# Graph network kernel: one-hots made a group ahead in the linear passes, group entries loaded early, and the first histogram made from two digits

## The chip, the cores and the metric

One core of a Trainium2 chip runs the whole program in one launch. The metric is device time in microseconds. The engines are PE (TensorE, matrix products), DVE (VectorE), ACT (ScalarE), POOL (GpSimd, which here mostly issues indirect DMAs) and SP (SyncE, which here issues plain DMAs). They run apart and meet at semaphores.

## The reference, cut to what matters

A graph of 12500 nodes (64 features each) and 200000 edges with one of 33 types and a weight passes through four networks in a row, each followed by a residual and a layer norm:

```
x = layernorm(x + L0(x, relations, edges, types))   # hyperbolic, 2 hops
x = layernorm(x + L1(x, edges, weights))            # GRU, 2 rounds
x = layernorm(x + L2(x, edges))                     # SAGE, 2 convolutions
x = layernorm(x + L3(x, edges))                     # SAGE, 2 convolutions
```

Each hop, round and convolution gathers the row of one end of every edge and adds it up at the other end (`segment_sum(x[row], col)`). In L0 the row goes through a chain of hyperbolic maps first; in the others it is only summed, and what is linear is done on the sums. Dst is sorted, src isn't.

## The kernel before, in words

**Sort.** The program first sorts the edges by the block of 128 nodes of their head, once by src (k = 0) and once by dst (k = 1). There are NB = 98 blocks. `make_hist` makes on DVE a bf16 one-hot of 98 columns for each of 40 edges a partition (125 partitions, so 3920 elements), `count` adds it over all edges on PE into `ps_total[k]`, and `starts(k)` turns the counts into where each block's tiles begin. For k = 0 that takes 40 one-hots ahead of `starts(0)`; for k = 1 they are made between the steps of the first sort. `rank` then gives each edge its place, and POOL scatters its entry (tail, head's place in the block, type, weight) with `L494`, 40 indirect DMAs a step, into `payload`, which SP has filled beforehand with empty entries (`L302`).

**Passes.** The sorted edges lie in 1664 tiles of 128, in 52 groups of G = 32 tiles. Eight passes go over them. Passes 0 and 1 (hyperbolic) have a loop of their own (`hyp_group`), with one-hots loaded from memory. Passes 2 to 7 are linear. All buffers of a group exist twice (h = 0, 1). In a linear pass, for each group:

- SP loads the group's entries into `pay[h]` (64 KB, `load_pay`, L326) once `rows_free` says that the group two before has been added;
- POOL waits for the entries and for `rows_free`, then issues 32 indirect DMAs (`gather`, L510), one a tile, that fetch the rows of the table into `rows[h]`;
- DVE makes the one-hots of the 32 tiles (`make_hot`, L1583, 128 x 4096 elements) from the entries;
- PE waits for the one-hots and for the gathered rows, then in `sum_group` for each half u of 16 tiles clears two banks (L745) and makes 16 products of a one-hot with its 64 columns of rows (L757, each recorded twice), and reports in `scattered`; pass 2 also makes a product for the weights (L760);
- DVE waits for the gathers and for each half's `scattered`, and adds the half into `acc` at a place read from a register (`add_half`, L1597), which it reports in `accumulated`. After the second it increments `rows_free`.

The order on DVE is one-hot of a group, its two adds, one-hot of the next. A DVE increment of `rows_free` by 2 opens each pass. Between passes come the dense steps, and SP stores the new table (`store_steps`, `store_normed`); `meet` is a barrier of all five engines. The order is that of each engine's instruction stream and its semaphores; `await_reg` is a wait on a value computed from the loop counter.

## Time and profile before

| | us |
|---|---|
| median of 3 runs | 31190.96 |
| lowest, highest | 31181.28, 31203.01 |
| profiled execution | 31202.25 |
| its span | 31200.5 |
| POOL busy | 16432.8 (53%) |
| PE busy, PE weight loads | 11983.8 (38%), 9990.2 (32%) |
| DVE busy | 8949.7 (29%) |
| ACT busy | 2075.3 (7%) |

Times inside the profile count from the span's start. "Idle before" is the time in which an engine did nothing ahead of an instruction, with what released it; "issue" means that the profile shows no release, "remote" one from another engine that it can't name. A line ends on the kernel's line number (L510). The start of a matrix product is recorded when it is issued, its end is modelled. Register and semaphore instructions are not shown.

### The profile page before, as it was taken

The numbers are of one execution on the slowest core, as the hardware profiler recorded it, in microseconds if no ns is written. First come the engines' busy times: TensorE is split into PE (matmuls) and PEld (weight loads), VectorE is DVE, ScalarE is ACT, GpSimd is POOL, SyncE is SP. The second block draws the span as 40 slices with busy tenths as digits, with TensorE's granted clock in tenths as the row PEclk, the third lists the DMA queues.
The fourth block names the chain that finished last, engine by engine and source line by source line (L and its number), as shares of the span: only waits on it lengthen the run. The fifth ranks groups of instructions, "written<-read, shape, count | busy, mean of one in ns | idle before, by whom it ended". The sixth has DMA issues, their size and how long they took to land. (4 is left out here: it accounts for less than half of the span.)

```text
span 31200.5 us, 205782 instructions
## 1 busy us (share of the span) xinstructions
PE 11983.8 (38%) x50453; PEld 9990.2 (32%) x50454; DVE 8949.7 (29%) x14216; ACT 2075.3 (7%) x3825; POOL 16432.8 (53%) x16724
## 2 busy tenths in 40 slices
PE   2222222245555555554444433433333332333333
PEld 1001111134444444443444422322222222323222
DVE  5334333345555455551111211211111111111111
ACT  0000000012222222220000000000000000000000
POOL 3555444445555455544444466456646655664665
PEclk5555555555555555555555555555555555555555
DMA  0000111222222222221000011011111111111111
GB/s 18 1 1 9 46 40 37 77 75 70 70 70 67 66 70 70 70 66 21 18 18 18 20 22 22 18 25 22 23 22 23 22 21 26 23 22 22 22 22 24
DMA packets 803016, 1093.26 MB, mean 35 GB/s; under 512 B 449066, under 2 KB 529390, under 8 KB 742884
## 3 DMA queue, kind: packets, MB, share of 16 engines
q0 software_dynamic: 528384, 511.86, 8.4%
q1 hardware_dynamic: 274404, 579.20, 5.3%
q14 instruction: 188, 1.54, 0.0%
q8 instruction: 40, 0.66, 0.0%
HBM read 877.63 MB, written 212.42 MB: 35 GB/s over the span
## 5 line engine op out<-in xcount | busy, mean ns | idle before, releaser
L510 POOL DMA_INDIRECT rows<-table_lin,pay x9984 | 9467.4, 948 | 7644.0 <-issue 3928.9
L757 PE MATMUL pair<-rows,onehot 128*128 128x64 f32 x19968 | 4927.2, 408 | 4645.8 <-issue 4644.8
L757 PEld LDWEIGHTS pair<-rows,onehot 128*128 128x128 f32 x19968 | 4644.6, 326 | 4925.2 <-issue 4924.9
L1597 DVE TENSOR_TENSOR acc<-acc,pair 128x1024 f32 x832 | 1016.1, 1221 | 14071.0 <-remote 10817.8
L510 POOL DMA_INDIRECT rows<-table_hyp,pay x3328 | 3450.0, 1037 | 1143.8 <-issue 985.1
L745 PE MATMUL pair<-ones_bf,zeros_bf 1*128 1x512 bf16 x1664 | 845.2, 602 | 5859.8 <-issue 5858.7
L719 PE MATMUL pair<-tab,sel_t 128*128 x6656 | 1687.3, 435 | 2991.0 <-ACT sel_t L960 2434.9
L494 POOL DMA_INDIRECT payload_dst<-rows x1600 | 1564.0, 977 | 1873.2 <-DVEq L1259 1397.6
L719 PEld LDWEIGHTS pair<-tab,sel_t 128*128 128x128 f32 x6656 | 1479.7, 327 | 3304.8 <-issue 3304.8
L494 POOL DMA_INDIRECT payload_src<-rows x1600 | 1558.6, 974 | 1413.8 <-issue 727.3
L745 PEld LDWEIGHTS pair<-ones_bf,zeros_bf 1*128 1x128 bf16 x1664 | 113.1, 100 | 6235.6 <-issue 6235.6
L1583 DVE TENSOR_TENSOR onehot<-pay,pair 128x4096 f32<-128x4096 int32 x312 | 1379.4, 4421 | 165.5 <-issue 165.5
L1245 DVE TENSOR_TENSOR rows<-pair,onehot 125x490 f32<-125x490 f32 x640 | 428.1, 669 | 2825.8 <-PE pair L575 1346.0
L579 PE MATMUL pair<-onehot,notbefore 125*125 125x490 bf16 x640 | 396.5, 620 | 2035.7 <-DVE rows L1245 1279.2
L760 PEld LDWEIGHTS pair<-rows,onehot 128*128 128x128 f32 x3328 | 913.8, 329 | 457.0 <-issue 456.9
L760 PE MATMUL pair<-rows,onehot 128*128 128x1 f32 x3328 | 863.5, 322 | 495.3 <-issue 495.2
L579 PEld LDWEIGHTS pair<-onehot,notbefore 125*125 125x125 bf16 x640 | 113.2, 177 | 2473.3 <-issue 2473.3
L520 POOL TENSOR_TENSOR rel<-rel,sc 128x1024 f32<-128x1024 f32 x104 | 196.3, 1908 | 1318.8 <-DVEq L1557 1318.8
L520 POOL TENSOR_TENSOR xs<-xs,sc 128x1024 f32<-128x1024 f32 x104 | 196.4, 1911 | 1281.9 <-DVEq L1557 1281.9
L710 PE MATMUL pair<-ident,onehot 128*128 128x128 f32 x3328 | 860.0, 421 | 26.4 <-DMA onehot<-head_hots 26.4
L1576 DVE TENSOR_TENSOR type_hot<-pay,pair 128x512 f32<-128x512 int32 x208 | 142.0, 683 | 2530.9 <-remote 2530.2
L1046 ACT COPY onehot<-pair 128x512 f32<-128x512 f32 x56 | 33.2, 592 | 11345.5 <-PE pair L809 5940.4
(307 smaller groups left out, 15201.5 us busy)
## 6 DMA issues: line engine op xcount, KB each, us to landing
onehot<-head_hots SPq DMA_DIRECT2D x208, 1024.0 KB
rows<-table_lin,pay POOLq DMA_INDIRECT x9984
rel<-rel_rows SPq DMA_DIRECT2D x52, 1072.0 KB
xs<-rel_rows SPq DMA_DIRECT2D x52, 1072.0 KB
head_hots<-msg SPq DMA_DIRECT2D x52, 1024.0 KB
head_hots<-onehot SPq DMA_DIRECT2D x52, 1024.0 KB
rows<-table_hyp,pay POOLq DMA_INDIRECT x3328
rel_rows<-rel SPq DMA_DIRECT2D x26, 1072.0 KB
```

The source lines that it names most:

```text
L494: pool.indirect_dma_start(out=payload[k][:, :], out_offset=bass.IndirectOffsetOnAxis(ap=addr[:, h, c:c + 1], axis=0), in_=stage[:, h, c, : ...
L510: pool.indirect_dma_start(out=rows[:, h, t, 0:width], out_offset=None, in_=table[:, :], in_offset=bass.IndirectOffsetOnAxis(ap=pay[:, h, t ...
L520: nc.gpsimd.tensor_tensor(rl, rl, over(EO[:, 3, half(u)], D), ALU.mult).then_inc(S["mixed", m], 1)
L579: nc.tensor.matmul(place[0:EP, 0:CH * NB], notbefore[0:EP, 0:EP], hot_c, start=False, stop=False, skip_group_check=True)
L710: last = nc.tensor.transpose(ps_sel[q % 2][:, j * P:j * P + P], onehot[:, h, 4 * q + j, :], ident[:, :])
L719: last = nc.tensor.matmul(ps_head[:, j * TW:j * TW + TW], sel_t[:, q % 2, j * P:j * P + P], flat_tab[:, bass.ds(b * TW, TW)], start=True, ...
L745: nc.tensor.matmul(sums[:, 512 * c:512 * c + 512], zeros_bf[0:1, :], ones_bf[0:1, :].unsqueeze(1).to_broadcast([1, 4, P]), start=True, sto ...
L757: last = nc.tensor.matmul(sums[:, bass.ds(at, D)], onehot[:, h, t, :], mv, start=False, stop=False, skip_group_check=True)
L760: nc.tensor.matmul(ps_weight[:, bass.ds(block_, 1)], onehot[:, h, t, :], rows[:, h, t, D:D + 1], start=False, stop=False, skip_group_check ...
L1245: V.tensor_tensor(picked, bank[1][0:EP, 0:CH * NB].rearrange("p (c b) -> p c b", b=NB), hist[:, h, c * CH:c * CH + CH, :], ALU.mult).then_ ...
L1583: V.tensor_tensor(onehot[:, h, :, :], over(pay[:, h, :, 1], P), ps_iota.unsqueeze(1).to_broadcast([P, G, P]), ALU.is_equal)
L1597: V.tensor_tensor(flat_acc[:, at], flat_acc[:, at], ps_half[u], ALU.add)
```

## The change

Three things are changed.

1. In the linear passes DVE makes the one-hot of group g + 1 before it waits for the sums of group g (a loop turned by half a group, with the first and last pieces outside).
2. SP loads the entries of the first two groups of a pass before the pass begins (`first_lists`, after the pass before or ahead of the table's stores). In the loop of the linear passes it waits no longer for `rows_free`, but, as the hyperbolic ones do, for the gathers that read the old entries and for the one-hot made from them.
3. The histogram of k = 0 no longer uses a one-hot of 98 columns. The block number is split into a high digit (13 values) and a low one (8 values). For 320 edges a partition at a time (five parts, two buffers) DVE makes two small one-hots, PE multiplies those of five edges by each other (65 x 40) and adds everything up in one bank. DVE picks the five diagonal blocks with a product with the identity, and one product with ones brings the counts to all partitions. The type and k = 1 keys are made after it.

In pass 2 the `scattered` increment moves from the last feature product to the last weight product.

```diff
--- before.py
+++ after.py
@@ -51,6 +51,10 @@
 HC = 40
 NCH = HC // CH
 GITERS = EC // HC // 2
+HI, LO = 13, 8
+PARTS = 5
+PC = EC // PARTS
+assert PC % CH == 0 and HI * LO >= NB
 KB = 7
 NITERS = NB // KB
 assert NITERS * KB == NB and NITERS % 2 == 0
@@ -163,6 +167,13 @@
         key_early = early.bitcast(I32)[0:EP, 0:EC]
         type_early = early.bitcast(BF16)[0:EP, 2 * EC:3 * EC]
         key_hot = early.bitcast(BF16)[0:EP, 0:HC * P].rearrange("p (c n) -> p c n", n=P)
+        hi_key = type_hot[:, :, :, :].rearrange("p a b c -> p (a b c)").bitcast(BF16)[0:EP, 0:EC]
+        lo_key = sel_t[:, :, :].rearrange("p a b -> p (a b)").bitcast(BF16)[0:EP, 0:EC]
+        digit_room = flat_hot.bitcast(BF16)[0:EP, 0:2 * PC * (HI + LO)].rearrange("p (h n) -> p h n", h=2)
+        hi_hot = digit_room[:, :, 0:PC * HI].rearrange("p h (c v) -> p h c v", v=HI)
+        lo_hot = digit_room[:, :, PC * HI:PC * (HI + LO)].rearrange("p h (c v) -> p h c v", v=LO)
+        by_class = flat_msg[0:CH * HI, 900:900 + CH * HI * LO]
+        ones_f = flat_msg[0:CH * HI, 1500:1500 + P]
         none_early = early.bitcast(BF16)[0:EP, 3 * EC:4 * EC]
 
 
@@ -196,6 +207,7 @@
         ps_sort_iota = bank[2][:, 3 * P:4 * P]
         ps_degree = [bank[7][:, P * k:P * k + NB] for k in range(2)]
         ps_total = [bank[0], bank[3]]
+        ps_digits = bank[4][0:CH * HI, 0:CH * LO]
         ps_q = [(bank[4], bank[5], bank[6]), (bank[0], bank[1], bank[2])]
 
 
@@ -208,6 +220,7 @@
         edges_here = sem("edges_here")
         filled = sem("filled")
         rows_here = sem("rows_here")
+        classes_ready = sem("classes_ready")
         stores = sem("stores")
         cleared = sem("cleared")
         x_again = sem("x_again")
@@ -359,23 +372,21 @@
                 for h in range(2):
                     store_rel(i, h)
 
+            def first_lists(k):
+                for h in range(2):
+                    load_pay(k, 0, h)
+
             def run_pass(m, k):
                 if m < 2:
                     for h in range(2):
-                        sp.wait_ge(rows_free, m * FREE + h + 1)
-                        load_pay(k, 0, h)
                         load_rel(0, h)
                         for u in range(2):
                             load_hot(m, 0, h, u, False)
-                with sp.Fori(1 if m < 2 else 0, ITERS) as i:
+                with sp.Fori(1, ITERS) as i:
                     for h in range(2):
 
-                        if m < 2:
-
-                            await_reg(sp, "sp", S["gathered", m][h], i * (G * 16))
-                            await_reg(sp, "sp", hot_made, 4 * i + (m * HOT + 2 * h - 2))
-                        else:
-                            await_reg(sp, "sp", rows_free, 2 * i + (m * FREE + h + 1))
+                        await_reg(sp, "sp", S["gathered", m][h], i * (G * 16))
+                        await_reg(sp, "sp", hot_made, 4 * i + (m * HOT + 2 * h - 2))
                         load_pay(k, i, h)
                         if m < 2:
 
@@ -428,10 +439,13 @@
                 for u in range(2):
                     sp.wait_ge(hot_moved[h][u], LOADED)
             meet(sp, BN["prep0"])
+            first_lists(0)
             run_pass(0, 0)
+            first_lists(0)
             store_steps(table_hyp, tab, S["q_kept", 1], 0)
             meet(sp, BN["hop0"])
             run_pass(1, 0)
+            first_lists(0)
 
             sp.wait_ge(cleared, 2)
             sp.dma_start(xs[:, 0:NB - 1, :], a["x"][0:(NB - 1) * P, :].rearrange("(b p) d -> p b d", p=P)).then_inc(x_again, 16)
@@ -456,18 +470,22 @@
             store_normed(0)
             meet(sp, BN["hop1"])
             run_pass(2, 0)
+            first_lists(0)
             store_steps(table_lin, y, S["blk_back", 10], 1)
             meet(sp, BN["gru0"])
             run_pass(3, 0)
+            first_lists(1)
             load_rowoff(1)
             store_normed(1)
             meet(sp, BN["gru1"])
             for l in range(2):
                 run_pass(4 + 2 * l, 1)
+                first_lists(1)
                 store_steps(table_lin, big, S["blk_back", 12], l * NITERS)
                 meet(sp, BN[f"c{l}a"])
                 run_pass(5 + 2 * l, 1)
                 if l == 0:
+                    first_lists(1)
                     store_normed(2)
                     meet(sp, BN["c0b"])
                 else:
@@ -651,15 +669,17 @@
                     nc.tensor.matmul(ps_rel[q % 2][:, 0:4 * RW], type_t[:, q, :], relblk[:, :, :].rearrange("p a b -> p (a b)"),
                                      start=True, stop=True).then_inc(rel_made, 1)
 
-            for h in range(2):
-                pe.wait_ge(S["count_hot", 0], h + 1)
-                count(0, hist, h, h == 0)
-            with pe.Fori(0, GITERS - 1) as i:
-                for h in range(2):
-
-                    await_reg(pe, "pe", S["count_hot", 0], 2 * i + (h + 3))
-                    count(0, hist, h, False)
-
+            for part in range(PARTS):
+                pe.wait_ge(S["count_hot", 0], part + 1)
+                for c in range(0, PC, CH):
+                    last = nc.tensor.matmul(ps_digits, hi_hot[:, part % 2, c:c + CH, :].rearrange("p c v -> p (c v)"),
+                                            lo_hot[:, part % 2, c:c + CH, :].rearrange("p c v -> p (c v)"),
+                                            start=part + c == 0, stop=False, skip_group_check=True)
+                last.then_inc(S["hist_counted", 0], 1)
+
+            pe.wait_ge(classes_ready, 1)
+            nc.tensor.matmul(ps_total[0][:, 0:CH * NB], ones_f, by_class.rearrange("p (c b) -> p c b", c=CH)[:, :, 0:NB],
+                             start=True, stop=True).then_inc(S["hist_counted", 0], 1)
             place_from_start(0)
             for h in range(2):
                 rank(0, 0, h)
@@ -757,8 +777,8 @@
                         last = nc.tensor.matmul(sums[:, bass.ds(at, D)], onehot[:, h, t, :], mv, start=False, stop=False,
                                                 skip_group_check=True)
                         if m == 2:
-                            nc.tensor.matmul(ps_weight[:, bass.ds(block_, 1)], onehot[:, h, t, :], rows[:, h, t, D:D + 1],
-                                             start=False, stop=False, skip_group_check=True)
+                            last = nc.tensor.matmul(ps_weight[:, bass.ds(block_, 1)], onehot[:, h, t, :], rows[:, h, t, D:D + 1],
+                                                    start=False, stop=False, skip_group_check=True)
                     last.then_inc(scattered, 1)
 
             def run_pass(m):
@@ -1202,7 +1222,14 @@
 
             def starts(k):
 
-                dve.wait_ge(S["hist_counted", k], 2 * GITERS)
+                if k == 0:
+                    dve.wait_ge(S["hist_counted", 0], PARTS)
+                    V.tensor_tensor(by_class.rearrange("p (c v w) -> p c v w", c=CH, v=HI),
+                                    ps_digits.rearrange("p (c w) -> p c w", c=CH).unsqueeze(2).to_broadcast([CH * HI, CH, HI, LO]),
+                                    ident[0:CH * HI, 0:CH * HI].rearrange("p (c v) -> p c v", c=CH).unsqueeze(3).to_broadcast([CH * HI, CH, HI, LO]),
+                                    ALU.mult)
+                    dve.drain().then_inc(classes_ready, 1)
+                dve.wait_ge(S["hist_counted", k], 2 * GITERS if k else PARTS + 1)
                 V.tensor_copy(count_f.rearrange("p c b -> p (c b)"), ps_total[k][:, 0:CH * NB])
                 dve.drain()
                 rsum(bucket[:, 1, :], count_f.rearrange("p c b -> p b c"))
@@ -1263,11 +1290,26 @@
                                 ps_sort_iota[0:EP, :].unsqueeze(1).to_broadcast([EP, HC, P]), ALU.is_equal)
                 dve.drain().then_inc(S["key_hot", k], 1)
 
+            V.memset(ones_f, 1.0)
             dve.wait_ge(src_here, 16)
+            V.tensor_scalar(key_early, edges_in[:, 0, :], 10, None, ALU.arith_shift_right)
+            dve.drain()
+            V.tensor_copy(hi_key, key_early)
+            dve.drain()
+            V.tensor_scalar(key_early, edges_in[:, 0, :], 7, LO - 1, ALU.arith_shift_right, ALU.bitwise_and)
+            dve.drain()
+            V.tensor_copy(lo_key, key_early)
+            dve.drain()
+            for part in range(PARTS):
+                h, cols = part % 2, slice(part * PC, part * PC + PC)
+                if part > 1:
+                    dve.wait_ge(S["hist_counted", 0], part - 1)
+                V.tensor_tensor(hi_hot[:, h, :, :], over(hi_key[:, cols], HI),
+                                ps_sort_iota[0:EP, 0:HI].unsqueeze(1).to_broadcast([EP, PC, HI]), ALU.is_equal)
+                V.tensor_tensor(lo_hot[:, h, :, :], over(lo_key[:, cols], LO),
+                                ps_sort_iota[0:EP, 0:LO].unsqueeze(1).to_broadcast([EP, PC, LO]), ALU.is_equal)
+                dve.drain().then_inc(S["count_hot", 0], 1)
             make_key(0)
-            for h in range(2):
-                make_hist(0, hist, h, h * HC)
-                dve.drain().then_inc(S["count_hot", 0], 1)
 
             dve.wait_ge(edges_here, 48)
             V.tensor_copy(type_early, edges_in[:, 2, :])
@@ -1276,13 +1318,6 @@
             stt(type_early, none_early, float(R), type_early, ALU.mult, ALU.add)
             V.tensor_copy(edges_in[:, 2, :], type_early)
             make_key(1)
-
-            with dve.Fori(0, GITERS - 1) as i:
-                for h in range(2):
-
-                    await_reg(dve, "dve", S["hist_counted", 0], 2 * i + (h + 1))
-                    make_hist(0, hist, h, i * (2 * HC) + (h + 2) * HC)
-                    dve.drain().then_inc(S["count_hot", 0], 1)
 
             starts(0)
             for h in range(2):
@@ -1649,13 +1684,19 @@
                     if m in (5, 7):
                         tt(y, y, b_c2[:, m // 2 - 2, :].unsqueeze(1).to_broadcast([P, NB, D]), ALU.add)
                         tt(y, y, xs, ALU.add)
-                    with dve.Fori(0, ITERS) as i:
-                        for h in range(2):
-                            make_hot(m, i, h)
-
-                            await_reg(dve, "dve", S["gathered", m][h], (i + 1) * (G * 16))
-                            add_sums(m, 2 * i + h)
-                            dve.sem_inc(rows_free, 1)
+                    def add_group(g):
+                        add_sums(m, g)
+                        dve.sem_inc(rows_free, 1)
+
+                    make_hot(m, 0, 0)
+                    with dve.Fori(0, ITERS - 1) as i:
+                        make_hot(m, i, 1)
+                        add_group(2 * i)
+                        make_hot(m, i + 1, 0)
+                        add_group(2 * i + 1)
+                    make_hot(m, ITERS - 1, 1)
+                    add_group(GROUPS - 2)
+                    add_group(GROUPS - 1)
                 meet(dve, BN[f"pass{m}"])
 
             def hop(k, n0):
```

## Rows read from the trace of the kernel before

**Rows 1.** By stage: window, length, busy of PE, PE loads, DVE, ACT, POOL; clock; DMA

```profile
219.00:6480.00 6261.00, 1508.46 (x6403) 765.40 (x6402) 2280.30 (x2537) 239.74 (x560) 3152.85 (x3232) 0.55 0.09 30
14120.00:17406.00 3286.00, 1556.67 (x6864) 1485.63 (x6864) 361.35 (x208) 0.00 (x0) 1567.82 (x1658) 0.50 0.09 18
17560.00:20164.00 2604.00, 860.56 (x3536) 759.99 (x3536) 354.56 (x156) 0.00 (x0) 1569.26 (x1659) 0.50 0.11 22
```

**Rows 2.** Page, part 5, the costliest group

```profile
L510 POOL DMA_INDIRECT rows<-table_lin,pay x9984 | 9467.4, 948 | 7644.0 <-issue 3928.9
```

**Rows 3.** Waits of POOL in pass 3

```profile
POOL rows L510 <- DMA pay<-payload_src: 508.6, 50, 17.0
```

**Rows 4.** Timeline of the start: SP, DVE, PE and POOL around the first histogram

```profile
12.23 0.98 DVE L1198 TENSOR_SCALAR head<-acc 125x1600 int32<-125x1600 int32 x1
...
83.57 0.38 SPq L302 DMA_DIRECT2D payload_dst<-msg  x1
...
212.14 4.24 DVE L1193 TENSOR_TENSOR onehot<-rows,pair 125x3920 bf16<-125x3920 f32 x1 [0.39 <-issue]
219.15 0.67 DVE L1206 COPY rows<-pair 128x490 f32<-128x490 f32 x1 [2.77 <-PE pair L559]
...
228.79 2.00 PE L568 MATMUL pair<-rows,ident 128*125 128x490 f32 x2 [9.68 <-DVEq L1229]
...
251.85 1.12 POOL L494 DMA_INDIRECT payload_src<-rows  x1 [251.40 <-issue]
```

**Rows 5.** Timeline of one group of pass 3 in order of time

```profile
20038.72 0.94 POOL L510 DMA_INDIRECT rows<-table_lin,pay  x1 [10.03 <-DMA pay<-payload_src]
...
20046.31 7.09 PE L757 MATMUL pair<-rows,onehot 128*128 128x64 f32 x32
...
20077.51 0.95 POOL L510 DMA_INDIRECT rows<-table_lin,pay  x1 [0.30 <-issue]
...
20084.13 1.22 DVE L1597 TENSOR_TENSOR acc<-acc,pair 128x1024 f32 x1 [13.00 <-remote]
20086.05 4.42 DVE L1583 TENSOR_TENSOR onehot<-pay,pair 128x4096 f32<-128x4096 int32 x1 [0.69 <-issue]
...
20088.55 0.95 POOL L510 DMA_INDIRECT rows<-table_lin,pay  x1 [10.09 <-DMA pay<-payload_src]
```

**Rows 6.** Page, part 6: a 64 KB transfer on SP's queue

```profile
payload_dst<-msg SPq DMA_DIRECT2D x52, 64.0 KB, 1.6
```

**Rows 7.** Timeline of the last group of pass 3, in which POOL issues nothing

```profile
20135.55 4.42 DVE L1583 TENSOR_TENSOR onehot<-pay,pair 128x4096 f32<-128x4096 int32 x1 [0.33 <-issue]
...
20144.98 1.00 PE L745 MATMUL pair<-ones_bf,zeros_bf 1*128 1x512 bf16 x2 [15.11 <-issue]
20145.91 7.09 PE L757 MATMUL pair<-rows,onehot 128*128 128x64 f32 x32
...
20162.29 1.22 DVE L1597 TENSOR_TENSOR acc<-acc,pair 128x1024 f32 x1 [7.40 <-PE pair L757]
```

**Rows 8.** Timeline of the first group of pass 5, after 64 gathers in a row

```profile
23182.09 0.95 POOL L510 DMA_INDIRECT rows<-table_lin,pay  x1 [0.30 <-issue]
...
23195.04 1.22 DVE L1597 TENSOR_TENSOR acc<-acc,pair 128x1024 f32 x1 [0.96 <-PE pair L757]
```

**Rows 9.** Timeline of one group of pass 0

```profile
8078.16 7.09 PE L757 MATMUL pair<-xs,onehot 128*128 128x64 f32 x32
...
8103.45 0.95 POOL L510 DMA_INDIRECT rows<-table_hyp,pay  x1 [0.30 <-issue]
...
8108.61 0.69 DVE L1576 TENSOR_TENSOR type_hot<-pay,pair 128x512 f32<-128x512 int32 x1 [25.63 <-remote]
```

**Rows 10.** Timeline of one group of pass 2

```profile
15080.53 0.94 POOL L510 DMA_INDIRECT rows<-table_lin,pay  x1 [0.30 <-issue]
...
15087.13 1.22 DVE L1597 TENSOR_TENSOR acc<-acc,pair 128x1024 f32 x1 [43.16 <-remote]
15100.41 1.22 DVE L1597 TENSOR_TENSOR acc<-acc,pair 128x1024 f32 x1 [12.06 <-PE pair L757]
```

## The prediction

> **What bounds the kernel now.** I read the stages first, then who waits in them, then single groups. Most of the time lies in eight passes over 52 groups of 32 tiles. The six linear passes (2 to 7) are alike but for pass 2, which makes twice as many products: 2604 us for pass 3, 3286 us for pass 2, or 50 and 63 us a group [rows 1]. No engine is full in pass 3: POOL is busy for 60% of it, PE for 33%, DVE for 14%. The costliest group of the page is POOL's issue of the gathers, with nearly as much idle time as work [rows 2]. An issue takes 0.95 us and the 0.30 us before the next never goes away, so 32 gathers cost 40.0 us. What could go is the wait once a group: 508.6 us in 50 waits, 10.2 us each, all put down to the payload [rows 3].
>
> One group shows what ends that wait [rows 5]. POOL begins at 20038.72 and ends its last issue at 78.46. The second add of the group before, on DVE, starts only at 84.13, 5.67 us later, and ends at 85.35. It frees the rows; then SP loads the payload, and POOL begins at 88.55. The period is 39.74 + 5.67 + 1.22 + 3.20 = 49.83 us.
>
> Why the add comes at 84.13 is the question. PE begins that group's products at 46.31. In the last group of the pass, with POOL silent, products from 20145.91 end in an add at 20162.29, 16.4 us [rows 7]; beside POOL it takes 37.8 us [rows 5]. And the end of the sums keeps to POOL's last issue: 5.67 us after it here; in pass 2, with twice the products, the first add comes 15087.13 − 15081.47 = 5.66 us after it, and the second 13.28 us later [rows 10]; in pass 0 PE has issued its last product of a sum at 8085.3, yet DVE, which waits for that sum, goes on only at 8108.61, 4.2 us after POOL's last issue ended at 8104.40 [rows 9]. I read this so: while POOL issues a batch, the ends of PE's sums are reported late, and the rest of them when the batch is over. The trace shows the pattern, not its cause.
>
> **The change part by part.**
> *One-hots a group ahead.* Today DVE makes a one-hot (4.42 us) after it has freed the group before, and PE's first product follows: 20135.55 to 45.91, 10.4 us [rows 7]. Afterwards the one-hot is made before DVE waits for the sums, so it leaves the path. PE is held next by the rows' landing. With some 1.6 us for that (taken from a 64 KB load [rows 6]) and the 5.9 us that PE took from a finished one-hot to its first product [rows 7], PE starts about when POOL starts the next batch, 7 to 8 us earlier than now. If the sums' end still keeps to POOL's last issue, those microseconds are worth nothing in passes 3 to 7: 0 per group, and bounds follow among the rivals. In pass 2 half the products still come after that moment; an earlier start lets a few more be issued before it. PE's second half took 13.28 us; I take off 0.8 (bounds 0 and 4).
>
> *Payload loaded early.* SP's load of a group no longer waits for the freed rows but for the landed gathers and the one-hot of two groups before. That is met some 1.6 us after POOL's last issue, and with as much again to load it lands by 4 us; the rows are free at 5.67 + 1.22 = 6.9 us. So it is hidden by 3 us, and if that cover went whole, the period would stay as now. What remains of the 3.20 us between the add's end and POOL's first issue is the semaphore and POOL's own start: below nothing it can't be, and 3.20 is today's. Taking off 2.2 us for SP's issue (0.33 to 0.38) and the load (1.6 to 1.9) leaves 1.0. The new period is 39.74 + 5.67 + 1.22 + 1.0 = 47.6 us. No wait is added ahead of DVE's adds but that for the next payload, long there; SP's queue holds only these loads in a linear pass. Before each pass two loads are issued ahead of the table's stores, under 1 us of SP's time beside waits for DVE.
>
> *Sum for a linear pass:* 50 gathers wait for freed rows, 50 × 2.2 = 110 us. In the last group PE need no longer wait for the one-hot after the release: 10 us of the 10.4. At the start the payload is there already, 2 us. That is 122 us, for passes 3 to 7 610 us. *Pass 2:* 50 × (2.2 + 0.8) + 12 = 162 us. *Passes 0 and 1:* only the start, 3 us; their loops stay. The increment that pass 2 moves to the weight product is worth 0.
>
> *First histogram.* Today 40 one-hots of 3920 elements go through DVE, 4.24 us each plus 0.39 idle at the last (0.55 on average by my estimate, since 40 of them and some 15 us of other work fill 12.23 to 219.15), 192 us, and DVE waits 2.8 us for the last count [rows 4]. New: five parts of 320 × 13 and 320 × 8 elements. At 4.24 us / 3920 = 1.08 ns that is 7.3 us, with a gap 7.6, so 38 us. The short rows of 13 and 8 are in no row here; if they halved the rate it would be 74 us, and faster than 38 I don't expect. Four more operations on 1600 elements are 4.2 us. DVE's by-class product of 520 elements is about 0.7 us, PE's product over 490 columns 2.0 us like the one at 228.79 [rows 4], 3 us with the hand-over. PE's 64 small products of a part hide under DVE's next part; left uncovered only the last shows. Saved: 192 + 3 − 38 − 4 − 3 = 150 us (bounds 110 and 155). POOL's first scatter moves from 251.85 to about 102, still behind the payload's fill, whose last issue is at 83.57 [rows 4]; the sort behind it is a chain through DVE, PE and POOL [rows 1] and moves as a whole. The memset of ones costs nothing: DVE waits there for the source indices.
>
> **Sum.** 610 + 162 + 3 + 150 = 925 us. The profiled execution took 31202.25 us (span 31200.5), 11 above the median of 31190.96: 31191 − 925 = 30266 us.
>
> **The rivals.**
> *A: the sums go on beside the gathers, only slower.* Then an earlier start is time won. The 5.67 us after the last issue do 5.67/16.4 of a sum and 32.15 us before it the rest, a rate of one sum in 49 us [rows 5, 7]. PE starts 47.3 us after its own gathers began (39.74 + 1.6 + 5.9), the next batch ends at T + 39.74, the add starts at 2T − 2.2: (T − 7.6)/49.2 + (T − 42.0)/16.4 = 1 gives T = 45.7 us. That is 4.1 × 50 + 12 = 217 us a pass, 1090 for five; pass 2 some 310; in all 1550 us, 29640 us. If a sum took 37.8 us wherever it lay, T would be 43.7 and the time 29140. For it speaks that PE's products after 20046 are slow, not stopped; against it, that three kinds of stage with different work end 4.2 to 5.7 us after POOL's last issue [rows 5, 9, 10].
> *A2: nothing but POOL bounds.* With sums of 16.4 us under the gathers the period is 32 × 1.25 = 40.0 us: 500 us a pass, in pass 2 1130, in all 3780 us, 27400 us. The same products beside gathers and alone speak against it [rows 5, 7]. The Trainium skill, SBUF — State Buffer, section "Who interferes with whom", says that DMA never contends with a compute engine and that PE waits on no one there; by that rule this rival would be the forecast. The rows disagree: 37.8 us against 16.4 for the same products.
> *B: the linear passes keep their period*, because the load or POOL's start is as late as ever (the 3.20 us are POOL's own). Left are the histogram and the last groups: 150 + 60 = 210 us, 30980 us.
> *C, slower: the shorter pause does not let the backlog go.* After 64 gathers in a row the second add came 23195.04 − 23183.04 = 12.0 us after the last issue, not 5.67 [rows 8]. If batches 8 us apart act like one long batch, the period is 39.74 + 12.0 + 1.22 + 1.0 = 54.0 us: 4.1 × 50 − 12 = 195 us lost a pass, 975 for five, 195 in pass 2, less 153: 32210 us. It decides from a lag of 8.6 us: (8.6 − 5.67 − 2.2) × 300 = 220, which eats the rest. Against it: after 32 gathers the lag is over in 5.7 us, and the new pause is 7.9.
>
> **How the numbers follow.** Forecast 0.52, A 0.27, A2 0.04, B 0.09, C 0.08. The forecast's own range is 30100 to 30550: the 1.0 us may be 0.4 or 1.8, 0.7 × 300, and the histogram 40. For eight in ten the range takes in A's main value and B: 29300 to 31000; A2, C and A's lower edge stay out. A change of 0.2%, 62 us, is about what can be told from none here. Faster holds in the forecast, A, A2 and B, 0.91 with a little off for an unseen wait; within 0.2% 0.02; slower 0.07.
>
> **What would show it.** The waits of POOL put down to the payload vanish; POOL's pause in pass 3 is near 8 us, ended by DVE; the second add stays 5.7 us behind POOL's last issue though PE's first product comes within 1 us of POOL's first issue (under A the add comes nearer or earlier; under C later). The one-hot's row lies before the adds. The last group of a pass follows its predecessor in some 18 us, not 28. DVE's first row of starts(0) lies near 69 us. Wrong I am if the add is free of POOL's batch, or if the lag grows.

## The result, and the profile after

The changed kernel takes 30162.93 us (median of 4 runs, 30151.55 to 30229.77) against 31190.33 for the kernel before on the same chip: a ratio of 0.9675 (95% interval 0.9658 to 0.9692), 1027 us less. Forecast were 30266 us, 925 us less, within 29300 to 31000. The profiled execution after is the slowest of its four: 30229.77 us, span 30228.0, 972.5 us under the profiled span before. Its other three runs took 30151.55 to 30171.30 us, so the split below is of an execution some 70 us longer than the others.

The stages, with the same columns as in [rows 1]: the sort, pass 2 and pass 3.

```profile
65.00:6338.00 6273.00, 1501.54 (x6347) 757.91 (x6346) 2279.54 (x2535) 235.00 (x552) 3115.88 (x3200) 0.55 0.09 30
13993.00:17000.00 3007.00, 1573.13 (x7011) 1512.54 (x7011) 381.60 (x240) 14.69 (x39) 1570.16 (x1664) 0.50 0.10 19
17112.00:19620.00 2508.00, 836.55 (x3536) 732.44 (x3536) 362.79 (x160) 0.00 (x0) 1570.00 (x1664) 0.50 0.12 23
```

The counts of instructions are nearly those of [rows 1]; only the lengths have changed: pass 3 by 96 us, pass 2 by 279 us in these windows, whose ends are not cut quite alike. From POOL's first gather of a pass to that of the next, read in the timeline of both profiled executions, the 972.5 us come out as follows:

| | before | after | difference |
|---|---|---|---|
| start to POOL's first scatter | 251.85 | 97.42 | 154.4 |
| from there to pass 0's first gather | 6188.4 | 6241.1 | −52.7 |
| passes 0 and 1 | 7671.5 | 7655.3 | 16.2 |
| pass 2, to pass 3's first gather | 3441.8 | 3118.6 | 323.2 |
| passes 3 to 7, to the end of the span | 13647.0 | 13115.6 | 531.4 |

The start, in the timeline of DVE and POOL (against [rows 4]):

```profile
16.80 4.49 DVE L1307 TENSOR_TENSOR onehot<-type_hot,pair 125x4160 bf16<-125x4160 bf16 x1
21.20 2.81 DVE L1309 TENSOR_TENSOR onehot<-sel_t,pair 125x2560 bf16<-125x2560 bf16 x1
...
62.31 0.70 DVE L1227 TENSOR_TENSOR msg<-pair,ident 65x520 f32<-65x520 f32 x1
65.13 0.67 DVE L1233 COPY rows<-pair 128x490 f32<-128x490 f32 x1 [2.12 <-PE pair L681]
...
97.42 1.12 POOL L512 DMA_INDIRECT payload_src<-rows  x1 [96.96 <-issue]
```

The forty one-hots of 3920 elements are gone. Five pairs of operations have come, 4.49 + 2.81 us each, 7.34 us from pair to pair, 36.7 us in all. The counts are copied out at 65.13 instead of 219.15, and POOL's first scatter follows 154.4 us sooner.

Waits of POOL in pass 3 (against [rows 3]), and then two of the costliest groups of the page (against [rows 2]):

```profile
POOL rows L528 <- DVEq L1689: 420.1, 50, 15.7
```

```profile
L528 POOL DMA_INDIRECT rows<-table_lin,pay x9984 | 9444.5, 946 | 6821.1 <-issue 3866.0
L777 PE MATMUL pair<-rows,onehot 128*128 128x64 f32 x19968 | 4790.2, 422 | 765.6 <-issue 765.6
```

No wait is put down to the payload any more. The 50 that are left end with L1689, where DVE gives the rows back, 8.4 us each instead of 10.2. The row of PE's products shows that an engine's idle time is no measure of gain. "Idle before" was 4645.8 us for the same 19968 products in the page of before, and it is 765.6 now: between two products of one sum PE hardly ever stands still. Almost 3900 us less idle time on an engine bought about 1000 us.

One group of pass 3, PE, POOL and DVE in order of time (against [rows 5]):

```profile
18643.62 7.09 PE L777 MATMUL pair<-rows,onehot 128*128 128x64 f32 x32
...
18644.57 0.94 POOL L528 DMA_INDIRECT rows<-table_lin,pay  x1 [8.28 <-DVEq L1689]
...
18651.37 1.22 DVE L1632 TENSOR_TENSOR acc<-acc,pair 128x1024 f32 x1 [2.92 <-issue]
18652.25 7.09 PE L777 MATMUL pair<-rows,onehot 128*128 128x64 f32 x32
...
18683.26 0.94 POOL L528 DMA_INDIRECT rows<-table_lin,pay  x1 [0.31 <-issue]
...
18690.23 1.22 DVE L1632 TENSOR_TENSOR acc<-acc,pair 128x1024 f32 x1 [37.64 <-remote]
18692.27 4.42 DVE L1618 TENSOR_TENSOR onehot<-pay,pair 128x4096 f32<-128x4096 int32 x1 [0.81 <-issue]
18692.41 0.94 POOL L528 DMA_INDIRECT rows<-table_lin,pay  x1 [8.20 <-DVEq L1689]
```

PE's first product is issued 0.95 us before POOL's first gather, not 7.6 us after it. The first half's add comes at once, at 18651.37. (Before, it came at 20069.91, 31.2 us into the batch: in [rows 5] the second add starts at 20084.13 after 13.00 us of idle time, and an add takes 1.22.) PE has issued the second half's last product by about 18659.3 (18652.25 + 7.09), and yet its add starts at 18690.23, 6.03 us behind the end of POOL's last issue (18683.26 + 0.94). The period is 39.63 + 6.03 + 1.22 + 0.96 = 47.84 us. Over pass 3 the medians are 49.76 us before and 47.90 after, with the add 5.70 and 6.08 us behind POOL's last issue.

The end of pass 3, DVE's last three adds (against [rows 7]), and one group of pass 2 (against [rows 10]):

```profile
19600.07 1.22 DVE L1632 TENSOR_TENSOR acc<-acc,pair 128x1024 f32 x1 [37.60 <-remote]
19609.14 1.22 DVE L1632 TENSOR_TENSOR acc<-acc,pair 128x1024 f32 x1 [7.85 <-PE pair L777]
19617.76 1.22 DVE L1632 TENSOR_TENSOR acc<-acc,pair 128x1024 f32 x1 [7.40 <-PE pair L777]
```

```profile
15068.80 0.94 POOL L528 DMA_INDIRECT rows<-table_lin,pay  x1 [16.64 <-DVEq L1689]
...
15088.57 0.36 PE L780 MATMUL pair<-rows,onehot 128*128 128x1 f32 x1 [1.25 <-issue]
15091.36 0.27 PE L777 MATMUL pair<-rows,onehot 128*128 128x64 f32 x1 [2.43 <-issue]
...
15107.50 0.94 POOL L528 DMA_INDIRECT rows<-table_lin,pay  x1 [0.30 <-issue]
...
15114.50 1.22 DVE L1632 TENSOR_TENSOR acc<-acc,pair 128x1024 f32 x1 [41.43 <-remote]
15123.55 1.22 DVE L1632 TENSOR_TENSOR acc<-acc,pair 128x1024 f32 x1 [7.83 <-PE pair L780]
...
15125.74 0.94 POOL L528 DMA_INDIRECT rows<-table_lin,pay  x1 [17.29 <-DVEq L1689]
```

The last group now ends 19617.76 − 19600.07 = 17.7 us behind the one before. In pass 2 the first add stands 6.06 us behind POOL's last issue (5.66 before); but the second follows it after 9.05 us, no longer 13.28 (medians of the pass: 8.85 and 12.67). PE's rows above tell of the limit that is left: some 20 us into POOL's batch they stop following each other closely; here the next one comes 2.8 us later.

### The profile page after: what moved, and what is told of

It is laid out like the page before. It is cut to its first block and busy times, and to the rows that moved or that the text cites. A ratio compares the mean times of both kernels' runs of the same rounds, so it can differ in the third digit from the quotient of the medians.

```text
span 30228.0 us, 205466 instructions
## 1 busy us (share of the span) xinstructions
PE 11768.9 (39%) x50455; PEld 9840.4 (33%) x50456; DVE 8821.3 (29%) x14192; ACT 2073.6 (7%) x3825; POOL 16385.0 (54%) x16724
## 2 busy tenths in 40 slices
DMA packets 803024, 1093.34 MB, mean 36 GB/s; under 512 B 449066, under 2 KB 529390, under 8 KB 742884
## 5 line engine op out<-in xcount | busy, mean ns | idle before, releaser
L777 PE MATMUL pair<-rows,onehot 128*128 128x64 f32 x19968 | 4790.2, 422 | 765.6 <-issue 765.6
L777 PEld LDWEIGHTS pair<-rows,onehot 128*128 128x128 f32 x19968 | 4502.7, 331 | 1289.0 <-issue 1288.7
L780 PEld LDWEIGHTS pair<-rows,onehot 128*128 128x128 f32 x3328 | 913.4, 329 | 602.2 <-issue 601.7
```

What stands on the lines that cost most here:

```text
L777: last = nc.tensor.matmul(sums[:, bass.ds(at, D)], onehot[:, h, t, :], mv, start=False, stop=False, skip_group_check=True)
L780: last = nc.tensor.matmul(ps_weight[:, bass.ds(block_, 1)], onehot[:, h, t, :], rows[:, h, t, D:D + 1], start=False, stop=False, skip_grou ...
```

## The experiments

L is the forecast's reading: in each batch (the gathers that POOL issues without a pause) the last sum is reported only behind POOL's last gather issue. A, A2 and C are the prediction's rivals. These runs were made on three other chips, on which the kernel before took 31693 us (the parts one by one), 31603 (rows by SP, half the gathers, fixed columns, rows by halves for the first time) and 31765 (plain loads, a quarter of the bytes, rows by halves for the second) and not 31190. Ratios compare runs of one chip. Pass lengths in this part count from POOL's first gather issue of a pass to its last. A batch's length and pauses are taken from one execution's trace.

### The three parts of the change, one by one

**The histogram alone.** The two-digit histogram in place of the one-hot of 98 columns, all else as before.

> The kernel before with the two-digit first histogram alone; nothing of the passes is changed. Both theories (L: the second half's sums end some 5.7 us behind POOL's last gather issue whatever PE does before; A: they go on beside the gathers, only slower) expect the same here. In the changed kernel POOL's first scatter of the sort came at 97.42 us instead of 251.85, 154 us earlier, so 31190 - 154 = 31036 us if the sort moves as a whole. In the changed kernel's profiled execution some 50 of the 154 us had been given back by the end of the sort; if that is the edit's own doing and not that one execution's, this kernel gains only about 100 us (31090). Linear period unchanged at 49.8 us.

31525.96 us, ratio 0.9948 (0.9932 to 0.9965): 167 us less than 31692.75. POOL's first scatter came at 97.19. The part is worth what the start showed.

**The early load alone.**

```diff
                 with sp.Fori(1, ITERS) as i:
...
-                            await_reg(sp, "sp", rows_free, 2 * i + (m * FREE + h + 1))
+                        await_reg(sp, "sp", S["gathered", m][h], i * (G * 16))
+                        await_reg(sp, "sp", hot_made, 4 * i + (m * HOT + 2 * h - 2))
```

> The kernel before with the early load of the payload alone: SP no longer waits for the freed rows; DVE still makes the one-hot after it has freed the rows. L: POOL's wait for the payload goes (2.2 us a group by the prediction, 1.9 by the changed kernel's period of 47.9), the lag behind POOL's last issue stays: period 47.6 to 47.9 us in passes 3 to 7, about 2 us less in pass 2's too, 300 x 1.9 = 570 us in all, 30620 us. A: POOL starts 2.2 us earlier, PE no earlier, so PE has 29.9 us beside the gathers instead of 32.15; 29.9/49.2 of a sum, and the rest at 16.4 a sum is 6.4 us: period 39.74 + 6.4 + 1.22 + 1.0 = 48.4 us, 420 us in all, 30770 us.

31631.27 us, ratio 0.9981 (0.9971 to 0.9990): only 61 us, a tenth of what L expected, and less than A's too. One group of pass 3, POOL, PE and DVE:

```profile
18660.87 0.94 POOL L515 DMA_INDIRECT rows<-table_lin,pay  x1 [9.91 <-DVEq L1663]
...
18671.08 7.09 PE L762 MATMUL pair<-rows,onehot 128*128 128x64 f32 x32
...
18685.98 0.27 PE L762 MATMUL pair<-rows,onehot 128*128 128x64 f32 x1 [1.83 <-issue]
18688.79 0.27 PE L762 MATMUL pair<-rows,onehot 128*128 128x64 f32 x1 [2.54 <-issue]
...
18699.65 0.94 POOL L515 DMA_INDIRECT rows<-table_lin,pay  x1 [0.31 <-issue]
...
18706.26 1.22 DVE L1602 TENSOR_TENSOR acc<-acc,pair 128x1024 f32 x1 [41.23 <-remote]
18708.31 1.22 DVE L1602 TENSOR_TENSOR acc<-acc,pair 128x1024 f32 x1 [0.82 <-issue]
...
18710.48 0.95 POOL L515 DMA_INDIRECT rows<-table_lin,pay  x1 [9.89 <-DVEq L1663]
```

POOL does start 0.95 us after the rows are free. But the one-hot comes behind that moment, so PE's first product is now 10.2 us behind POOL's first gather. From 18683.9 on PE issues one product instruction (a product is recorded as two) every 2.1 to 2.8 us for a while, and the first half's sum, which [rows 5] had out some 14 us before the other, is reported behind the batch as well. The two adds now stand one behind the other: 39.72 + 5.67 + 2.05 + 1.22 + 0.95 = 49.6 us. Part of this was there without the load: with the histogram alone, whose linear loops are those of the kernel before, both adds lie behind the batch in 36 of 49 batches of 32 gathers in pass 3 on this chip, with the load in all 49. Against that kernel (period 50.3 us, last add 6.3 us behind the batch, POOL's start 3.1 us after the add's end) the load wins 2.2 us at POOL's start and pays back 1.4 at the add, which comes 7.75 us behind the batch. In pass 2 the lateness costs more than the load gives: 3422.1 us from first to last gather against 3354.6 with the histogram alone.

**The one-hots ahead alone.**

```diff
-                    with dve.Fori(0, ITERS) as i:
-                        for h in range(2):
-                            make_hot(m, i, h)
...
+                    make_hot(m, 0, 0)
+                    with dve.Fori(0, ITERS - 1) as i:
+                        make_hot(m, i, 1)
+                        add_group(2 * i)
+                        make_hot(m, i + 1, 0)
+                        add_group(2 * i + 1)
```

> The kernel before with the one-hots made one group ahead alone; SP's load still waits for the freed rows. PE can begin its products some 6 us earlier in each group. L: the second half's add stays 5.7 us behind POOL's last issue, the period of passes 3 to 7 stays at 49.8 us; gained are only the last group of each pass (28.3 to 17.7 us in the changed kernel, 5 x 10.6 = 53, and 10 in pass 2) and pass 2's second half, which stood 13.3 us behind and 9.1 in the changed kernel, 50 x 3.8 = 190: about 250 us in all, 30940 us. A: with the sums running on beside the gathers, (T - 7.6)/49.2 + (T - 44.2)/16.4 = 1 gives a period of 47.3 us, 2.5 x 250 = 625 us more than L, about 30300 us.

30963.99 us, ratio 0.9768 (0.9752 to 0.9784): 729 us less, in total nearer to A's 890 than to L's 250. The stages say otherwise. One regular group of pass 3:

```profile
18773.00 0.94 POOL L510 DMA_INDIRECT rows<-table_lin,pay  x1 [19.04 <-DMA pay<-payload_src]
...
18779.49 1.22 DVE L1597 TENSOR_TENSOR acc<-acc,pair 128x1024 f32 x1 [2.91 <-PE pair L757]
...
18811.69 0.94 POOL L510 DMA_INDIRECT rows<-table_lin,pay  x1 [0.30 <-issue]
...
18818.76 1.22 DVE L1597 TENSOR_TENSOR acc<-acc,pair 128x1024 f32 x1 [38.05 <-remote]
...
18823.04 0.94 POOL L510 DMA_INDIRECT rows<-table_lin,pay  x1 [10.40 <-DMA pay<-payload_src]
```

In passes 3 to 7 it is L's picture: the add 6.1 us behind POOL's last issue, a period of 50.0 us (the median of pass 3 is 50.1, with the histogram alone 50.3). A's 47.3 us is not there. Pass 3 is 2556.5 us long against 2601.8 with the histogram alone; L had nothing for that. The regular group brings little of these 45 us: now and then a pause is shorter (the mean period of the batches of 32 is 49.4 us), and four more batches run on to 64 gathers. Over passes 3 to 7 this is 243 us. The larger gain that L had put too low is in pass 2: 2946.0 us against 3354.6, 409 us and not 200. With both parts pass 2 takes 2956.7 us, so there the whole gain comes with this part and the load adds nothing: without the early load POOL starts 2.7 us behind PE's first product and not 0.8 (medians), and PE has that time to itself.

**The changed kernel, again.**

> The changed kernel again, for a second profiled execution. Its time is 30163 us as before. Open is whether the 51 us that the profiled sort gave back over its 80 batches (lead over the kernel before 154 us at the first, 103 at the last) belong to the kernel: that execution took 30229.8 us, the three others 30151.6 to 30171.3. If it was that execution's own, this profile shows a lead near 150 us at the end of the sort and a span near 30155; if the kernel's, again about 100.

30500.48 us, ratio 0.9626 (0.9610 to 0.9642). From the first scatter to pass 0's first gather the profiled executions on this chip took 6413.7 (this one), 6446.1 (histogram alone), 6429.6 and 6440.5 us (the two with the old histogram). That is a spread of some 30 us with no difference between the old histogram and the new. So nothing here ascribes to the edit the 52.7 us that the sort seemed to give back on the first chip; that execution was some 70 us longer than its fellows. The parts alone save 0.5, 0.2 and 2.3%, 3.0% together; the whole saves 3.7%. In pass 3 the load alone takes off 34.8 us, the one-hots alone 45.3, both 110.8 (2491.0 us).

### What holds PE back

**No work of POOL: rows by SP.**

```diff
+            def rows_sp(m, i, h):
+                await_reg(sp, "sp", rows_free, 2 * i + (m * FREE + h + 1))
+                for t in range(G):
+                    sp.dma_start(rows[:, h, t, 0:D], table_lin[t * P:t * P + P, :]).then_inc(S["gathered", m][h], 16)
```

> The changed kernel, but in passes 2 to 7 the rows of a group are brought by 32 plain DMAs that SP issues (the table's rows in order, so the indirection is left out and the sums are of other rows), and POOL issues nothing there. As many bytes go into the same buffers. L (it is POOL's issuing that holds back PE): the sum of a group takes some 16.4 us again, no add comes 5.7 us after anything, and the period is set by PE, 17 to 20 us; five passes of 50 groups then lose about 250 x 28 = 7000 us, in all near 22000 us with pass 2. Rival T (it is the rows' traffic into SBUF that slows PE's sums to 37.8 us): the period stays at 38 us or more, 27500 us or more.

21887.92 us, ratio 0.6927 (0.6907 to 0.6947). The same bytes, brought by plain DMAs, do not slow PE: a sum takes 16.4 us again. L holds against T.

**Plain loads issued by POOL.**

```diff
                 for t in range(G):
+                    if m > 2:
+                        pool.dma_start(rows[:, h, t, 0:D], table_lin[t * P:t * P + P, :]).then_inc(S["gathered", m][h], 16)
+                        continue
                     pool.indirect_dma_start(
```

> The changed kernel, but in passes 3 to 7 POOL issues 32 plain loads of rows in order in place of the 32 indirect gathers (the sums are of other rows). Same engine, same bytes, no indirection. If it is any DMA issued by POOL that holds PE back, the second half's add stays some 5.5 us behind POOL's last issue, and the period is 32 issues + 8. If it is the indirect ones alone, the lag goes, the sum takes 16.4 us beside POOL, and the period is that of POOL's issues alone or of PE's 17.5 to 20 us, whichever is longer.

23659.5 us, ratio 0.7449 (0.7434 to 0.7464). A group of pass 3, POOL, PE and DVE:

```profile
18025.72 16.83 POOL L529 DMA_DIRECT2D rows<-table_lin  x32 [6.82 <-DVEq L1692]
...
18026.24 7.09 PE L780 MATMUL pair<-rows,onehot 128*128 128x64 f32 x32
18034.00 1.22 DVE L1635 TENSOR_TENSOR acc<-acc,pair 128x1024 f32 x1 [4.18 <-PE pair L780]
18034.86 7.09 PE L780 MATMUL pair<-rows,onehot 128*128 128x64 f32 x32
18042.63 1.22 DVE L1635 TENSOR_TENSOR acc<-acc,pair 128x1024 f32 x1 [7.41 <-PE pair L780]
```

POOL's 32 issues, 0.53 us each, run beside all 64 product instructions, and the adds are put down to PE's products and follow them: 18034.00 and 18042.63, 16.4 us behind the first product, as in [rows 7] with POOL silent. So it is not POOL's issuing as such. It is something of the indirect ones. Two weaker readings are out as well. The batch is shorter (16.83 us), but the next one follows after 2.04 us, at 18044.59, and PE's products in it are issued without gaps too, from 18049.81. And the number and size of the packets are the same: the page of the changed kernel and the page of this one both have 803024 packets and 1093.34 MB. Not told apart is the order of the rows: the plain loads read them one behind the other, the gathers all over the table.

**A quarter of the bytes.**

```diff
-                        out=rows[:, h, t, 0:width], out_offset=None, in_=table[:, :],
+                        out=rows[:, h, t, 0:16], out_offset=None, in_=table[:, :].rearrange("n (a b) -> (n a) b", b=16),
```

> The changed kernel, but each gather of passes 3 to 7 brings only 16 of a row's 64 numbers (from other rows of the same table; the other 48 are summed as they lie in the buffer). POOL issues as many gathers, of a quarter of the bytes. L in the form 'POOL's issuing holds PE's reports': issue time and lag unchanged, period 47.9 to 48.1 us. Rival Q, 'PE's report waits until the queue of gathers has been worked off' (it came 2 us behind the landing of the last rows): with fewer bytes the rows land sooner, and the add moves forward with them, by up to 2 us: period 46 to 47 us.

30570.76 us, against 30572.26 for the changed kernel on the same chip; in pass 3 the medians of the period (48.1 us) and of the lag (6.3 us) are the same in both. Bytes play no part. Q itself was not put to the test: the rows land no earlier with a quarter of the bytes, 1.27 us behind POOL's last issue (median) against 1.28. The add comes 5.0 us behind that landing, not 2 as I had it. Against Q speak the two runs with other batches below: the add comes 2.8 us behind the last landing after 16 gathers and 7.3 us after 48, no fixed distance.

**Fixed columns in place of registers.**

```diff
+                        else:
+                            at = j * D
```

> The changed kernel, but in passes 3 to 7 PE's products take fixed columns (tile j of a half into columns 64 j) instead of addresses worked out from registers, and PE loads no block numbers (the sums go to other blocks). It tells what in PE is slow beside POOL's gathers. If it is the register work between the products (the records show 0.7 us for it in place of 0.07): PE's products are no longer slow, and if the lag of the second half's add hangs on it too, the period falls to 40 to 43 us. If the lag is the report of the last product alone (L in its narrow form): the changed kernel already issues its products within 15.6 us, and the period stays at 48 us.

30461.21 us, ratio 0.9640 (0.9612 to 0.9668); the changed kernel has 0.9626 and 0.9624 on the two other chips. The time is the same, the rhythm isn't. DVE and POOL in pass 3:

```profile
18592.36 1.22 DVE L1636 TENSOR_TENSOR acc<-acc,pair 128x1024 f32 x1 [25.52 <-remote]
18592.44 0.94 POOL L528 DMA_INDIRECT rows<-table_lin,pay  x1 [0.30 <-issue]
...
18650.56 1.22 DVE L1636 TENSOR_TENSOR acc<-acc,pair 128x1024 f32 x1 [51.74 <-remote]
...
18656.21 0.95 POOL L528 DMA_INDIRECT rows<-table_lin,pay  x1 [16.53 <-DVEq L1693]
```

POOL issues 64 gathers in a row in 22 of the batches behind the first, and pauses 16.4 us on average after them; 96.4 us for 64 are 48.2 for 32. The second half of the first of the two groups is added in the midst of such a batch (at 18592.36, 32 us into it; 30 to 40 us in 21 of the 22), so POOL need not stop after 32. The last add of the other group stands some 14 us behind the last issue. This is against L as I had worded it: a sum can be reported while POOL issues, only late. What the run does show is that the register work is not what makes PE slow: PE's idle time ahead of these products is back at 4850.5 us in this page, as much as before the change, and the kernel is no slower for it. Whether the lag hangs on it can't be read from this run, since the batches are others; why they are was not followed up.

### How the lag goes with the batch

**Half the gathers.**

```diff
-                for t in range(G):
+                for t in range(HG if m > 2 else G):
```

> The changed kernel, but in passes 3 to 7 POOL gathers only the first 16 of a group's 32 tiles (the other half is summed from rows left in the buffer). PE and DVE do the same work. L: the second add stays tied to POOL's last issue, whatever that batch's length: 16 x 1.25 = 19.9, + 5.5 lag + 1.2 + 1.0 = 27.6 us a group, 20.3 us less than the changed kernel: 250 x 20.3 = 5070 us less, near 25100 us by the first chip's time. Rival A (the sum itself takes 37.8 us beside gathers): with half the gathers 19.9 us slow (0.4 of a sum) and 0.6 x 16.4 = 9.8 us after them, 31.9 us. If the sum took 37.8 us whatever POOL does, 40 us or more.

24788.49 us, ratio 0.7845. A group of pass 3:

```profile
18016.06 0.94 POOL L528 DMA_INDIRECT rows<-table_lin,pay  x1 [6.13 <-DVEq L1689]
...
18034.78 0.94 POOL L528 DMA_INDIRECT rows<-table_lin,pay  x1 [0.30 <-issue]
...
18039.76 1.22 DVE L1632 TENSOR_TENSOR acc<-acc,pair 128x1024 f32 x1 [12.58 <-remote]
...
18041.93 0.94 POOL L528 DMA_INDIRECT rows<-table_lin,pay  x1 [6.20 <-DVEq L1689]
```

The period is 25.9 us. The add moved with POOL's last issue, as L has it and A (31.9) hasn't; but the lag is 4.0 us, not the 5.5 that I had put in. It goes with the length of the batch. (Medians of pass 3: period 25.8 us, lag 4.0.)

**Rows given back by halves.** Run on two chips, on the second beside the changed kernel.

```diff
-                        add_sums(m, g)
+                        for u in range(2):
+                            sum_made(m, g, u)
+                            add_half(m, g, u)
+                            dve.sem_inc(half_free, 1)
...
+                    if m > 1 and t % HG == 0:
+                        await_reg(pool, "pool", half_free, 4 * i + ((m - 2) * (2 * GROUPS + 4) + 2 * h + t // HG + 1))
```

> The changed kernel, but the rows are given back by halves: DVE counts up after each half's add, and POOL waits before tile 0 and before tile 16 instead of once for the whole group. L (PE's report comes late for as long as POOL issues): POOL gains nothing by it, since the second half's count is only out some 5.5 us after POOL has stopped; the period stays at 48 us, or grows towards 2 x (19.9 + 5.5 + 1.2 + 1.0) = 55 us if POOL now has to stop twice a group. Rival A (sums go on beside gathers, slower): POOL's pauses shrink, 44 to 46 us. Rival A2 (POOL alone bounds once it may run on): 40 us, 250 x 8 = 2000 us faster.

> Rows given back by halves again, now in three rounds beside the changed kernel on the same chip. Its first look gave 30075.6 us against 31603.3 for the kernel before (ratio 0.952, the changed kernel's own 0.963 to 0.968). If that holds it takes 1.0 to 1.5% less than the changed kernel, mean period of passes 3 to 7 46.9 us against 47.9, of pass 2 about 50 to 51 against 56 to 57.

> The changed kernel beside it, for the comparison: ratio to the kernel before between 0.9626 and 0.9675, as on the two chips so far.

30075.57 us the first time, ratio 0.9518 (0.9490 to 0.9546); the second time 30150.22 us, ratio 0.9491 (0.9475 to 0.9507), against 30572.26, ratio 0.9624 (0.9608 to 0.9640), for the changed kernel. So it is 422 us or 1.4% faster than the changed kernel, the fastest of the kernels here that leave nothing out. One batch of pass 3:

```profile
18634.84 0.94 POOL L532 DMA_INDIRECT rows<-table_lin,pay  x1 [10.87 <-DVEq L1695]
...
18680.76 1.01 PE L769 MATMUL pair<-ones_bf,zeros_bf 1*128 1x512 bf16 x2 [26.07 <-issue]
...
18693.51 0.94 POOL L532 DMA_INDIRECT rows<-table_lin,pay  x1 [0.30 <-issue]
...
18702.82 1.22 DVE L1636 TENSOR_TENSOR acc<-acc,pair 128x1024 f32 x1 [50.79 <-remote]
...
18704.99 0.94 POOL L532 DMA_INDIRECT rows<-table_lin,pay  x1 [10.54 <-DVEq L1695]
```

The add of a half no longer holds POOL back when the buffer's other half is free. Behind the first 64 gathers pass 3 is 33 batches of 48 (in about half of them with a stop of 1.9 us behind the first gather) and a last one of 16. The add that ends its pause comes 8.4 us behind the last issue (18693.51 + 0.94), and the pause is 10.5 us. A2's 40 us a group is far off. L's 48 to 55 us and A's 44 to 46 both miss: 48 gathers in 70.15 us are 46.8 us for 32, and 47.4 on the mean of the pass. The number of pauses falls, and each grows. For pass 3, without its first batch:

| gathers in a batch | pause of POOL, median, us | mean period, us | for 32 gathers |
|---|---|---|---|
| 16 (half the gathers) | 6.1 | 26.1 | 52.1 |
| 32 (the changed kernel) | 8.5 | 48.1 | 48.1 |
| 48 (rows by halves) | 10.7 | 71.1 | 47.4 |
| 64 (fixed columns) | 16.5 | 96.4 | 48.2 |

Longer batches win less than the pauses suggest, and nothing more at 64. Most of the gain is in pass 2: 2666.0 us long against 2967.0, with batches that are shorter than before (29 of 32 gathers, 42 of 16); there a half's gathers need no longer wait for the other half's sum. Pass 3 is 2459.3 us against 2491.5. Of the 427 us between the two profiled executions 297 lie between the first gathers of passes 2 and 3, and 129 behind.

The trace also settles a rival that I had not put down. In the changed kernel PE, when it has issued the last product of a group, waits for the rows of the next, and they are complete 1.2 us behind POOL's last issue; so the late sum might only be one that PE reports when it goes on. Here PE goes on to the next group at 18680.76 (it clears a bank), and the sum before that is added at 18702.82, 22 us later. So it is not PE's own next step that the report waits for.

## Why the prediction was right

- *The period of passes 3 to 7: right.* Forecast 39.74 + 5.67 + 1.22 + 1.0 = 47.6 us, measured 39.63 + 6.03 + 1.22 + 0.96 = 47.84. Three terms hold within 0.11 us; the lag is 0.36 us longer. In this group the period fell by 1.99 us and not 2.2. Over passes 3 to 7 the time from first to last gather fell by 479.5 us for 550, which is 70 of the 79 us by which they gained less than forecast (531 for 610).
- *"Those microseconds are worth nothing in passes 3 to 7": nearly right alone, wrong beside the load.* Alone, the one-hots ahead leave the period at 50.0 us, with 45 us a pass from other rhythms. But two thirds of the load's 2.2 us exist only with them: alone it gave 49.6 us. The sum was right because both edits were made; its split was not. What I had overlooked is that PE issues at its full rate only in the first 20 us or so of a batch. As I read the rows, an earlier POOL without an earlier PE moves the first half's sum past the batch, and DVE then adds twice on the path.
- *Pass 2: the term that was mis-sized.* Forecast 3.0 us a group; from first to last gather the pass fell from 3230.5 to 2925.3 us, 305/51 = 6.0 a group, in all 323 us for 162. PE's second half was to take 0.8 us less, and it took 13.28 − 9.05 = 4.2 less in the groups shown, beyond the bound of 4 that I had kept, and 12.67 − 8.85 = 3.8 less by the medians, just within it. "An earlier start lets a few more be issued" was the step: each microsecond of the earlier start is one at PE's full rate (two product instructions in 0.85 us with their two for the weights), and those it replaces, late in the batch, held one instruction in 2 to 3 us. It fits that this gain comes with the one-hots alone, and that the load's 2.2 us, which I had added for pass 2, bring nothing beside them there.
- *The histogram: right.* 36.7 us for 38, the first scatter 154 us earlier for 150; alone it saved 167 us on another chip.
- *The total is nearer than its parts, and that is luck.* Against 925 us stand 972.5 in the profiled executions: 161 more in pass 2 and 13 more in passes 0 and 1, 79 less in passes 3 to 7 and 48 less from the start to pass 0's first gather.
- *Rival A* fell in its numbers with the period of 50.0 and 25.9 us, but not whole: sums do get out beside the gathers, late, as with the fixed columns 30 to 40 us into the batch. L's "only behind the last issue" is a rhythm of the 32-gather batches and not a rule. *A2* fell with the rows by halves, *B* with the waits of POOL. The Trainium skill, SBUF — State Buffer, section "Who interferes with whom", would have made A2 the forecast. For plain loads the runs agree with its rule (16.4 us a sum beside POOL's 32 issues); beside indirect gathers a second half whose products are issued within 8 us is reported after 38.
- *Rival C* had one part right and missed the other, which set its price: the lag does grow with the gathers that POOL issues in a row, but the batches 8.3 us apart did not act like one long batch.

What would show it: the payload's waits, the place of the add and the 17.7 us at a pass's end came as foretold. DVE's copy of the counts was foretold near 69 us and came at 65.13.

**What stays open** is the cause itself: why the indirect gathers, and neither POOL's plain loads in order nor the bytes nor PE's registers, make PE slow, and why its last sum comes late. The runs bound it from outside only, and no run made plain loads of rows out of order.

## What to carry to other kernels

When an engine's work ends at a fixed distance behind another engine's last issue, read the pause per batch before shortening the work: PE's idle time fell by almost 3900 us here, and the kernel gained what the path gained. Two edits on one loop are costed together, and each alone, since the first may only move what the second needs; the load here was worth 35 us in pass 3 alone and 65 beside the other. If a pause comes once in a batch, ask whether finer releases let the issuer go on sooner: that was worth another 1.4%, most of it in the pass where PE had most to do.

## What the runs showed of the hardware

- 32 indirect gathers in a row by POOL (0.95 us and a gap of 0.30) hold PE's last sum back until 6.0 us after the last one; 16 until 4.0 us, 48 until 8.4 us. 32 plain loads of as many bytes and packets (0.53 us each), of rows in order, do nothing of the kind.
- It is no hard stop: with fixed columns a half's sum was added 30 to 40 us into a batch of 64 gathers.
- PE issues its products at full rate for the first 17 to 23 us of such a batch and then one instruction in 2 to 3 us, whether it began before the batch (pass 2 after the change: 17.3 us, median) or 10 us into it (the early load alone, pass 3: 21.7 us).
- The same kernel took 31190 us on one chip and 31603, 31693 and 31765 us on three others. The difference lies in part in the sort, 6188 us on the first against some 6430 on the chip with 31693.
